# Table weights decoded by masks and predicated copies, and small inputs requested a stage earlier, in a four-layer fp32 kernel

## The chip, the cores and the metric

The kernel runs as one program on one core of one Trainium2 chip. The metric is the device time of the whole program in microseconds (us). Engines: TensorE (PE, its weight loads are PEld), VectorE (DVE), ScalarE (ACT), GpSimd (POOL) and SyncE (SP, which issues most of the transfers). They run in parallel, each takes its own instructions in order, and they wait for each other on semaphores.

## What is computed

A stack of four layers on x, 1024 tokens of 256 numbers in fp32. Each layer is a feed-forward, an attention and the feed-forward again, each behind a layer norm:

```python
x = x + 0.5 * _L0_ffn_ref(_layernorm(x), lut, gate_idx, up_idx, down_idx)
x = x + _L0_attn_ref(_layernorm(x), ...)          # 16 heads of 16, (q.k)^4, causal
x = x + 0.5 * _L0_ffn_ref(_layernorm(x), ...)
# layer 1: mixture of 8 experts, latent attention;  layer 2: mixture of 64 experts, gated delta rule
# layer 3: 4-bit feed-forward with 1024 hidden, attention on pooled keys

def _ghost_linear(x, idx, lut):
    w = lut[idx]                                   # lut has 16 entries
    return jnp.einsum('bsh,oh->bso', x, w)
gate = _ghost_linear(x, gate_idx, lut)             # gate_idx, up_idx [688, 256]
up = _ghost_linear(x, up_idx, lut)
h = jax.nn.silu(gate) * up
return _ghost_linear(h, down_idx, lut)             # down_idx [256, 688]
```

The weights of layer 0's feed-forward are thus given as integers from 0 to 15 and a table of 16 numbers. In layer 2's attention a small projection (`Wa`, `Wb`, with biases) gives the decay and the step size of each head and token, and then 16 heads are computed one after another, each with its own 512 KB of weights and a short convolution. Layer 3's attention multiplies keys with two pooling vectors, picks its heads by a matrix of head rows and pools windows of 16 keys by a window matrix.

## The kernel before

The tokens are 8 tiles of 128. The program is a series of stages (`Stage`); at the end of each all engines meet at a barrier, and the next stage's instructions, its transfers on SP among them, start behind it. A transfer issued inside a stage is therefore waited for inside that stage, unless it was issued by an earlier stage into a buffer that outlives it (`prefetch` of `norm_stage`, `idle` of the feed-forward stages, `AttentionWeights.load`).

**Layer 0, first feed-forward** (`l0_decode_ffn_stage`). The 688 hidden columns are cut into 6 units of 115 (padded). A unit's weights are 716 columns on 128 partitions: 460 for gate and up (`IN0`), 256 for down. They are decoded from the integers `idx` while earlier units are multiplied. For each of the 16 table entries VectorE makes the entry's value where the integer equals it and zero elsewhere (lines 460 and 474, `is_equal` then `mult`, 96 of them), and adds two or three of such results (lines 487 and 490, 51 adds). TensorE sums the 7 to 10 terms of a unit with the identity as weights (line 384, `decode`) in PSUM, and ScalarE copies the sum into `w` (line 437, `keep`). The products of a unit are `up` (line 395, gate and up of one half of the tokens), silu on ScalarE (line 445), `mix` on VectorE (line 498) and `down` (line 402). The order is written out by hand: up half 0, decode, up half 1, decode, down half 0, decode, down half 1. The decoded `w` is used again by the second feed-forward of the layer.

**Layer 0, attention.** After the head norm, `turn_stage` transposes q and k (line 656) and copies them out with a scale and a shift per partition, `columns` (lines 669 and 682), requested by the stage itself. The stage of the heads requests the matrix `own` (head rows) itself and multiplies it into the keys (line 1007).

**Layer 2, attention.** A norm, then `l2_decay_stage` (requests `w` and `row` at lines 2021 and 2022; its 16 products at line 2032 wait for both; then a chain of sigmoid, exp, ln and sums up to the table of decays), then `l2_heads_stage`, which requests gain and offset, the convolution taps and the weights of heads 0 and 1 and the first row of decays (lines 2251 to 2266) at its own start; line 2296 is its projection, 2528 and 2529 bring it to SBUF, line 2875 on GpSimd needs the row of decays.

**Layer 3, attention.** `l3_attention`'s last stage requests `taste`, `rows` and `inside` (lines 3662 to 3664); lines 3759 on GpSimd and 3780 on VectorE wait for all three.

## Time and profile before

| | |
|---|---|
| median of 3 runs | 2238.65 us (2233.58 to 2244.4) |
| the profiled execution, its own time | 2245.68 us |
| its span in the profile | 2244.0 us |
| PE busy | 1899.6 us, 85% |
| DVE, ACT, POOL busy | 1234.8, 840.0 and 471.7 us |
| granted TensorE clock, mean | 0.91 |

The span runs from the first to the last instruction; the profiled execution took 1.7 us more than it, and lies 7 us above the median. Shares of the span are means over many stages with different limits, so each stage has to be read by itself. A group of rows gives the time that instructions of one line were busy, the mean of one, and the idle time of the engine just before them with what ended it. "issue" there means that nothing the profile shows was waited for. The granted clock is 1.00 at TensorE's full 2.4 GHz and 0.50 at 1.2 GHz.

### The profile page before, as it was taken

To read this page: it belongs to the slowest core of one execution; us is meant where nothing else is said; L and a number is where in the kernel's file an instruction comes from. 1 tells how busy PE (TensorE), PEld (TensorE's weight loads), DVE (VectorE), ACT (ScalarE), POOL (GpSimd) and SP (SyncE) were. 2 spreads that over 40 slices of the span, in tenths; PEclk is the share of its full clock that TensorE was granted. 3 is DMA by queue.
4 is the path that set the end of the run, shared out by engine and by line. 5 is a ranking of instruction groups with operands and counts; after the bars stand their busy time and mean duration, and the time that the engine had idled before them with its cause. 6 is when DMAs were issued, how large, how long until landed. Compare 5 with 4: busy or idle time off the path is not lost. (4 is left out here: it accounts for less than half of the span.)

```text
span 2244.0 us, 52270 instructions
## 1 busy us (share of the span) xinstructions
PE 1899.6 (85%) x21231; PEld 1311.7 (58%) x21233; DVE 1234.8 (55%) x3231; ACT 840.0 (37%) x1977; POOL 471.7 (21%) x536
## 2 busy tenths in 40 slices
PE   7996779895999896676899999999998797679569
PEld 3444654563777563553666766676676674446456
DVE  7957641434663446644566666676666326542642
ACT  1013321221652222233667667767765202220120
POOL 0002410321000332641121222122121003720200
PEclk9997999996999997787999999999999697789679
DMA  7000000422400516761010001001000317730000
GB/s 267 13 0 1 1 1 0 154 68 89 179 1 3 189 38 206 234 229 41 21 41 22 21 22 41 21 22 41 22 30 14 84 26 232 247 149 7 3 3 19
DMA packets 55330, 157.37 MB, mean 70 GB/s; under 512 B 12899, under 2 KB 29881, under 8 KB 50822
## 3 DMA queue, kind: packets, MB, share of 16 engines
q1 hardware_dynamic: 45206, 128.84, 17.3%
q0 software_dynamic: 9888, 25.20, 3.4%
q8 instruction: 171, 2.80, 0.5%
q14 instruction: 65, 0.53, 0.1%
HBM read 115.36 MB, written 40.48 MB: 69 GB/s over the span
## 5 line engine op out<-in xcount | busy, mean ns | idle before, releaser
L2296 PE MATMUL l_heads_ps_p<-xnT,l2a_w 128*128 128x512 f32 x512 | 260.9, 625 | 22.0 <-DMA l2a_w<-in_l_w_heads 8.2
L2702 DVE SCALAR_TENSOR_TENSOR l_heads_taps<-l_heads_padded,l_heads_conv,l_heads_taps 128x1024 f32<-128x1024 f32 x144 | 187.5, 1321 | 11.0 <-ACT l_heads_taps L2529 10.0
L2296 PEld LDWEIGHTS l_heads_ps_p<-xnT,l2a_w 128*128 128x128 f32 x512 | 85.8, 191 | 83.9 <-issue 50.3
L198 PE MATMUL norm_turn<-zeros,ident 128*128 128x512 f32 x120 | 68.2, 726 | 52.9 <-PEq L60 52.9
L2875 POOL TENSOR_TENSOR l_heads_e<-l2a_table,l_heads_row 128x512 f32<-128x512 f32 x32 | 33.4, 1044 | 330.9 <-DVE l_heads_first L2713 325.7
L189 ACT ACT_TABLE_LOAD x10 | 12.8, 1283 | 205.3 <-PEq L60 205.3
L198 PEld LDWEIGHTS norm_turn<-zeros,ident 128*128 128x128 f32 x120 | 26.9, 233 | 88.3 <-issue 88.3
L2528 ACT COPY l_heads_padded<-l_heads_ps_p 128x512 f32<-128x512 f32 x96 | 57.2, 596 | 53.3 <-PE l_heads_ps_p L2296 53.3
L2529 ACT ACTIVATE l_heads_taps<-l_heads_ps_p,l_heads_conv 128x512 f32<-128x512 f32 x96 | 76.8, 800 | 0.0
L1905 ACT ACTIVATE l_heads_e<-l_heads_logit,l_heads_shift 128x128 f32<-128x128 f32 (+1 forms) x128 | 56.6, 443 | 44.6 <-DVE l_heads_shift L1937 44.6
L2878 POOL TENSOR_SCALAR_AFFINE_SELECT l_heads_e<-l_heads_e 128x512 f32<-128x512 f32 x64 | 67.6, 1056 | 9.8 <-POOL l_heads_e L2875 0.6
L384 PE MATMUL l_ffn_a_ps_w<-l_ffn_a_term,ident 128*128 128x512 f32 (+1 forms) x180 | 59.9, 479 | 9.0 <-DVE l_ffn_a_term L487 9.0
L2713 DVE SCALAR_TENSOR_TENSOR l_heads_first<-l_heads_bank,l2a_table,l_heads_e 128x128 f32<-128x128 f32 x128 | 36.0, 344 | 52.6 <-issue 46.1
L2330 PE MATMUL l_heads_bank<-l_heads_mt,l_heads_mz 32*32 32x32 f32 x3072 | 49.9, 194 | 13.9 <-issue 13.8
L2875 POOL TENSOR_TENSOR l_heads_e<-l_heads_row,l2a_table 128x512 f32<-128x512 f32 x32 | 34.4, 1074 | 118.7 <-DVE l_heads_qk L2755 118.7
L384 PEld LDWEIGHTS l_ffn_a_ps_w<-l_ffn_a_term,ident 128*128 128x128 f32 x180 | 33.8, 195 | 40.4 <-issue 28.5
L1019 DVE TENSOR_TENSOR l_heads_fourth<-l_heads_squares 128x768 f32<-128x768 f32 x32 | 31.0, 968 | 35.8 <-POOL l_heads_squares L915 35.8
L2330 PEld LDWEIGHTS l_heads_bank<-l_heads_mt,l_heads_mz 32*32 32x32 f32 x3072 | 41.5, 107 | 15.5 <-issue 15.4
L2603 ACT ACTIVATE l_heads_k_end<-l_heads_bank,l2a_table 128x128 f32<-128x128 f32 x128 | 36.8, 376 | 35.5 <-PE l_heads_bank L2436 35.5
L1937 DVE CUSTOM_DVE_ANT_0 l_heads_logit<-l_heads_ps_s,l_heads_mask 128x256 f32<-128x256 f32 (+1 forms) x128 | 40.3, 353 | 16.6 <-PE l_heads_ps_s L1837 16.5
L2773 DVE TENSOR_SCALAR l_heads_on<-l_heads_o,l_heads_mean_var,l_heads_rstd 128x128 f32<-128x128 f32 x128 | 35.6, 342 | 21.7 <-POOL l_heads_rstd L2888 21.2
L979 ACT ACTIVATE l_heads_squares<-l_heads_ps_s 128x768 f32<-128x768 f32 x32 | 26.0, 811 | 55.7 <-PE l_heads_ps_s L931 55.7
(706 smaller groups left out, 4868.9 us busy)
## 6 DMA issues: line engine op xcount, KB each, us to landing
l_results<-zeros SPq DMA_DIRECT2D x24, 512.0 KB, 5.3
l_ffn_a_w_in<-in_l_in_w SPq DMA_DIRECT2D x8, 1536.0 KB, 10.4
l_ffn_b_w_in<-in_l_in_w SPq DMA_DIRECT2D x8, 1536.0 KB, 11.1
l2a_w<-in_l_w_heads SPq DMA_DIRECT2D x16, 512.0 KB, 3.8
l_heads_row<-l_rows SPq DMA_DIRECT2D x16, 512.0 KB, 5.1
l_ffn_a_w_out<-in_l_out_w SPq DMA_DIRECT2D x8, 768.0 KB, 9.2
l_ffn_a_w_in<-l_results SPq DMA_DIRECT2D x8, 768.0 KB, 7.0
l_ffn_b_w_out<-in_l_out_w SPq DMA_DIRECT2D x8, 768.0 KB, 9.4
```

Source lines behind the costliest of these rows:

```text
L198: pe.matmul(turn[:, i % KC, (i // KC) % HALVES, :], core.ident[:], core.zeros[:, 0:HALF], start=True, stop=True)
L384: mm = pe.matmul(bank[:, 0:at.stop - at.start], core.ident[:], term[n % SLOTS][:, at], start=(m == 0), stop=(m == len(operands(u)) - 1))
L1905: act.activation(e[m % 4][:, lo:hi], logit[m % 4][:, lo:hi], ACT.Exp, bias=shift[:, m % 4, j:j + 1], scale=-1.0, accum_out=total[:, n % 4, ...
L1937: dve.tensor_tensor_reduce(logit[m % 4][:, lo:hi], score_bank(n, j)[:, i * width:(i + 1) * width], mask[:, 2 * P - width:], -1.0, LARGEST, ...
L2296: mm = pe.matmul(ps_p[half][:], w[b][:, which, c, :], core.xnT[:, c, half * HALF:(half + 1) * HALF], start=(c == 0), stop=(c == KC - 1))
L2330: mm = pe.matmul(bank[c][1][q, s, 0:BK], m_first(c, s)[q, q] if n == 1 else mz[c][q, s, 0, :], mt[c][q, s, :], start=True, stop=True)
L2528: act.copy(padded[which][:, 2 * half:2 * half + 2, PAD:], src)
L2529: act.activation(taps[which][:, 2 * half:2 * half + 2, :], src, ACT.Identity, bias=conv[b][:, which, TAPS:TAPS + 1], scale=conv[b][:, whic ...
L2603: last = act.activation(dst[:, s, :], tile_of_bank[name][:, s, :], ACT.Copy, scale=columns(h, column, c)[:, s:s + 1])
L2702: dve.scalar_tensor_tensor(out=taps[which][:], in0=padded[which][:, :, j:j + SEQ], scalar=conv[p % 2][:, which, j:j + 1], in1=taps[which][ ...
L2875: pool.tensor_tensor(m[:], a, b, ALU.subtract).then_inc(gap_ready, 1)
L2878: pool.affine_select(out=m[:], in_=m[:], compare_op=(ALU.is_gt, ALU.is_ge)[which], fill=DONE_BEFORE, base=0, pattern=[[0, SY], [-sign, P]] ...
```

## The change

**Decoding.** The table lookup is now a tree of choices on half a unit (358 columns), so there are 12 steps `v`. ScalarE folds the integer three times (lines 470, 474 and 478, absolute value of itself less a constant), makes an integer of all ones or zero from the last fold (`odd`, line 485), and three masks into PSUM (lines 493, 499 and 503, relu, nonzero where the choice falls the other way). VectorE makes 8 leaves: each is a pair of neighbouring table entries, chosen by the last bit with `and` and `xor` on the bits (line 547). Then 7 predicated copies join them: 4 by the outer mask, 2 by the high one, 1 by the tall one (line 562), and the last result lies in `w`. The identity products, the copies out of PSUM and the terms are gone. The two PSUM banks that held the sums now hold the masks, and the last half unit's gate and up use them. The padding entry is now 0 and `down` reads 113 rows of the last unit. TensorE's order is up half 0, down half 1 of the unit before, up half 1, down half 0; its first product of a unit waits for both steps of it.

**Requests.** A class `Asked` holds small tensors, their semaphore and their load; `columns` and `own` of layer 0, gates' weights and bias, gain and offset, and the first two heads' taps and weights of layer 2, and the three small tensors of layer 3 are now issued one stage or more ahead: in the first feed-forward of layer 0, in the norm before layer 2's decay stage, and in the first feed-forward of layer 3. The first row of decays stays where it was, in the stage of the heads.

```diff
+LEAVES = LUT // 2
+def folded_bits(entry):
+    first = abs(entry - (LUT - 1) / 2)
+    second = abs(first - LUT / 4)
+    third = abs(second - LUT / 8)
+    return entry >= LUT // 2, first < LUT / 4, second < LUT / 8, third < LUT / 16
...
             def up(u, h):
-                pe.wait_ge(w_ready, 2 * (u + 1))
-                if 2 * u + h >= 1:
+                pe.wait_ge(joined, joined_by(2 * u + 1))
+                if 2 * u + h >= 1 and banks(u, h) is not ps_mask:
                     pe.wait_ge(hidden_ready, 2 * u + h)
...
             for u in range(UNITS0):
-                more = u + 1 < UNITS0
                 up(u, 0)
-                if more:
-                    decode(u + 1, 0)
+                if u > 0:
+                    down(u - 1, 1)
                 up(u, 1)
...
+            def fold_index(v):
+                if v % 2 == 0:
+                    act.wait_ge(idx_loaded[v // 2], 32)
+                if v > 0:
+                    act.wait_ge(mask_ready[HIGH], v)
+                act.activation(fold[0][:], idx[:, v // 2, columns(v)], ACT.Abs, bias=middle).then_inc(folded, 1)
...
+            def make_leaves(v):
+                dve.wait_ge(odd_ready, v + 1)
+                if v > 0:
+                    dve.wait_ge(joined, joined_by(v - 1))
+                for k in range(LEAVES):
+                    set_entry = 2 * k if folded_bits(2 * k)[3] else 2 * k + 1
+                    other = 4 * k + 1 - set_entry
+                    dve.tensor_scalar(leaf_of(v, k).bitcast(I32), odd[v % 2][:], flips[:, k:k + 1],
+                                      table[:, other:other + 1].bitcast(I32), ALU.bitwise_and, ALU.bitwise_xor)\
+                        .then_inc(leaf_ready, 1)
+            def join(v, wanted):
...
+                    dve.copy_predicated(leaf_of(v, into), mask(bit).bitcast(I32), leaf_of(v, taken)).then_inc(joined, 1)
...
             for u in range(UNITS0):
-                more = u + 1 < UNITS0
-                if more:
-                    make_terms(u + 1, 0)
-                mix(u, 0)
...
+                for h in range(HALVES):
+                    v = 2 * (u + 1) + h
+                    if v < STEPS:
+                        make_leaves(v)
+                        join(v, OUTER)
+                    mix(u, h)
+                    if v < STEPS:
+                        join(v, HIGH)
+                        join(v, TALL)
...
+class Asked:
+    def __init__(self, nc, ctx, name, shapes):
+        self.at = [ctx.enter_context(nc.sbuf_tensor(f"{name}_{tensor}", shape, F32)) for tensor, shape in shapes]
+        self.loaded = nc.alloc_semaphore(f"{name}_loaded")
+        self.all = 16 * len(shapes)
+    def load(self, sp, *sources):
+        for at, source in zip(self.at, sources):
+            sp.dma_start(at[:], source).then_inc(self.loaded, 16)
...
+                def load_first(sp):
+                    gates.load(sp, w_gates.rearrange("(c p) n -> p c n", p=P), b_gates.partition_broadcast(P))
+                    first_w.load(sp, conv, conv_heads, w, w_heads)
+                    affine.load(sp, ln_w.rearrange("(d a) -> d a", a=1), ln_b.rearrange("(d a) -> d a", a=1))
+                norm_stage(nc, core, prefetch=load_first)
+                l2_decay_stage(nc, core, gates, table, rows)
```

VectorE in the first feed-forward of layer 0, before, between two `mix` instructions (`l_ffn_a_hidden`); `l_ffn_a_term` and `l_ffn_a_second` are looked-up values of a whole unit:

```order
L498 TENSOR_TENSOR l_ffn_a_hidden_217<-l_ffn_a_gate,l_ffn_a_ps_up 115x512 [waits l0_ffn_a_silu_done_217]
L460 TENSOR_SCALAR l_ffn_a_term_217<-l_ffn_a_idx,l_ffn_a_table 128x716 [waits l0_ffn_a_term_summed_217]
L460 TENSOR_SCALAR l_ffn_a_second_217<-l_ffn_a_idx,l_ffn_a_table 128x716 [waits l0_ffn_a_term_ready_217]
L490 TENSOR_TENSOR l_ffn_a_term_217<-l_ffn_a_term_217,l_ffn_a_second_217 128x716 [waits l0_ffn_a_looked_up_217]
L460 TENSOR_SCALAR l_ffn_a_second_217<-l_ffn_a_idx,l_ffn_a_table 128x716 [waits l0_ffn_a_term_ready_217]
L487 TENSOR_TENSOR l_ffn_a_term_217<-l_ffn_a_term_217,l_ffn_a_second_217 128x716 [waits l0_ffn_a_added_217,l0_ffn_a_looked_up_217]
L460 TENSOR_SCALAR l_ffn_a_term_217<-l_ffn_a_idx,l_ffn_a_table 128x716 [waits l0_ffn_a_term_summed_217]
L460 TENSOR_SCALAR l_ffn_a_second_217<-l_ffn_a_idx,l_ffn_a_table 128x716 [waits l0_ffn_a_added_217]
L487 TENSOR_TENSOR l_ffn_a_term_217<-l_ffn_a_term_217,l_ffn_a_second_217 128x716 [waits l0_ffn_a_looked_up_217]
L498 TENSOR_TENSOR l_ffn_a_hidden_217<-l_ffn_a_gate,l_ffn_a_ps_up 115x512 [waits l0_ffn_a_silu_done_217]
```

The same engine and place now, again from one `mix` to the next; `l_w` is the leaf that ends as the weights, `l_ffn_a_ps_mask` a mask in PSUM:

```order
L568 TENSOR_TENSOR l_ffn_a_hidden_217<-l_ffn_a_gate,l_ffn_a_ps_up 115x512 [waits l0_ffn_a_silu_done_217]
L562 COPY_PREDICATED l_w<-l_ffn_a_ps_mask_217,l_ffn_a_leaf_217 128x358 [waits l0_ffn_a_joined_217,l0_ffn_a_mask_ready1_217]
L562 COPY_PREDICATED l_ffn_a_leaf_217<-l_ffn_a_ps_mask_217,l_ffn_a_leaf_217 128x358 [waits l0_ffn_a_joined_217,l0_ffn_a_mask_ready1_217]
L562 COPY_PREDICATED l_w<-l_ffn_a_ps_mask_217,l_ffn_a_leaf_217 128x358 [waits l0_ffn_a_joined_217,l0_ffn_a_mask_ready0_217]
L547 TENSOR_SCALAR l_w<-l_ffn_a_odd_217,l_ffn_a_flips,l_ffn_a_table 128x358 [waits l0_ffn_a_joined_217,l0_ffn_a_odd_ready_217]
L547 TENSOR_SCALAR l_ffn_a_leaf_217<-l_ffn_a_odd_217,l_ffn_a_flips,l_ffn_a_table 128x358 x7
L562 COPY_PREDICATED l_w<-l_ffn_a_ps_mask_217,l_ffn_a_leaf_217 128x358 [waits l0_ffn_a_leaf_ready_217,l0_ffn_a_mask_ready2_217]
L562 COPY_PREDICATED l_ffn_a_leaf_217<-l_ffn_a_ps_mask_217,l_ffn_a_leaf_217 128x358 [waits l0_ffn_a_leaf_ready_217,l0_ffn_a_mask_ready2_217] x3
L568 TENSOR_TENSOR l_ffn_a_hidden_217<-l_ffn_a_gate,l_ffn_a_ps_up 115x512 [waits l0_ffn_a_silu_done_217]
```

A wait of VectorE for TensorE's sums (`term_summed`) is gone, and 15 instructions of 358 columns stand between two `mix`, where 8 of 716 stood here (12.5 on average over a unit's two halves).

TensorE in the same stage, before, from one pair of gate and up (line 395) to the next:

```order
L395 MATMUL l_ffn_a_ps_gate<-xnT,l_w 115x512 x2
L395 MATMUL l_ffn_a_ps_up<-xnT,l_w 115x512 x2
L384 MATMUL l_ffn_a_ps_w_217<-l_ffn_a_term_217,ident 128x512
L384 MATMUL l_ffn_a_ps_w_217<-l_ffn_a_term_217,ident 128x204
L384 MATMUL l_ffn_a_ps_w_217<-l_ffn_a_term_217,ident 128x512
L384 MATMUL l_ffn_a_ps_w_217<-l_ffn_a_term_217,ident 128x204
L402 MATMUL l_ffn_a_ps_down_217<-l_ffn_a_hidden_217,l_w 128x512 x2
L384 MATMUL l_ffn_a_ps_w_217<-l_ffn_a_term_217,ident 128x512
L384 MATMUL l_ffn_a_ps_w_217<-l_ffn_a_term_217,ident 128x204
L384 MATMUL l_ffn_a_ps_w_217<-l_ffn_a_term_217,ident 128x512
L384 MATMUL l_ffn_a_ps_w_217<-l_ffn_a_term_217,ident 128x204
L402 MATMUL l_ffn_a_ps_down_217<-l_ffn_a_hidden_217,l_w 128x512 x2
```

And now:

```order
L431 MATMUL l_ffn_a_ps_gate<-xnT,l_w 115x512 [waits l0_ffn_a_hidden_ready_217,l0_ffn_a_joined_217]
L431 MATMUL l_ffn_a_ps_gate<-xnT,l_w 115x512
L431 MATMUL l_ffn_a_ps_up<-xnT,l_w 115x512 x2
L439 MATMUL l_ffn_a_ps_down_217<-l_ffn_a_hidden_217,l_w 128x512 [waits l0_ffn_a_hidden_ready_217]
L439 MATMUL l_ffn_a_ps_down_217<-l_ffn_a_hidden_217,l_w 128x512
```

No identity product is left between them; what TensorE waits for at the start of a unit is the last predicated copy.

## Rows read from the trace of the kernel before

**Rows 1.** Busy time by engine, middle of the first feed-forward stage; columns: us, PE, PEld, DVE, ACT, POOL, granted clock, DMA share, GB/s.

```profile
40.00:130.00 90.00, 90.00 (x249) 44.89 (x248) 82.30 (x127) 9.24 (x18) 0.00 (x0) 1.00 0.20 79
```

**Rows 2.** Groups by line, 20 to 148.2 us; columns: xcount, busy us, mean ns, idle before.

```profile
L384 PE MATMUL l_ffn_a_ps_w<-l_ffn_a_term,ident 128*128 128x512 f32 (+1 forms) x180 | 59.9, 479 | 9.0 <-DVE l_ffn_a_term L487 9.0
L487 DVE TENSOR_TENSOR l_ffn_a_term<-l_ffn_a_term,l_ffn_a_second 128x716 f32<-128x716 f32 x41 | 37.1, 904 | 1.4
L460 DVE TENSOR_SCALAR l_ffn_a_second<-l_ffn_a_idx,l_ffn_a_table 128x716 f32<-128x716 int32 x51 | 29.9, 586 | 0.0
L395 PE MATMUL l_ffn_a_ps_gate<-xnT,l_w 128*115 128x512 f32 x48 | 22.7, 595 | 2.4 <-DVE l_ffn_a_hidden L498 1.5 <-ACT l_w L437 0.9
L498 DVE TENSOR_TENSOR l_ffn_a_hidden<-l_ffn_a_gate,l_ffn_a_ps_up 115x512 f32<-115x512 f32 x12 | 8.3, 688 | 17.7 <-ACT l_ffn_a_gate L445 17.4
```

**Rows 3.** Timeline, end of that stage; columns: start us, length us.

```profile
137.77 1.94 PE L395 MATMUL l_ffn_a_ps_gate<-xnT,l_w 128*115 128x512 f32 x4 [1.50 <-DVE l_ffn_a_hidden L498]
...
141.27 3.60 PE L402 MATMUL l_ffn_a_ps_down<-l_ffn_a_hidden,l_w 115*128 115x512 f32 x8
...
146.71 1.28 DVE L520 SCALAR_TENSOR_TENSOR x<-l_ffn_a_ps_w,x 128x512 f32<-128x512 f32 x2
```

**Rows 4.** Timeline of VectorE at the start of that stage.

```profile
20.62 0.59 DVE L460 TENSOR_SCALAR l_ffn_a_term<-l_ffn_a_idx,l_ffn_a_table 128x716 f32<-128x716 int32 x1 [6.22 <-DMA l_ffn_a_idx<-in_l_out_idx]
21.13 0.59 DVE L460 TENSOR_SCALAR l_ffn_a_second<-l_ffn_a_idx,l_ffn_a_table 128x716 f32<-128x716 int32 x1
21.75 0.91 DVE L487 TENSOR_TENSOR l_ffn_a_term<-l_ffn_a_term,l_ffn_a_second 128x716 f32<-128x716 f32 x1
22.57 0.59 DVE L474 TENSOR_SCALAR l_ffn_a_term<-l_ffn_a_idx,l_ffn_a_table 128x716 f32<-128x716 int32 x1
```

**Rows 5.** Single lines with operands per partition: shortest/median/longest ns.

```profile
L180 DVE TENSOR_SCALAR norm_xn<-x,norm_mean_var,norm_rstd x64: 401/407/414, 9.3 to 2182.5; 128x256 f32<-128x256 f32 x64
...
L2773 DVE TENSOR_SCALAR l_heads_on<-l_heads_o,l_heads_mean_var,l_heads_rstd x128: 336/341/348, 1133.3 to 1772.2; 128x128 f32<-128x128 f32 x128
...
L3544 ACT ACTIVATE l_ffn_a_hidden<-l_ffn_a_ps_up,l_ffn_a_bias x8: 687/687/688, 2019.5 to 2041.6; 128x512 f32<-128x512 f32 x8
```

**Rows 6.** Busy time and granted clock around two pauses of TensorE in layer 2.

```profile
1220.40:1222.10 1.70, 0.10 (x12) 0.00 (x0) 0.62 (x3) 1.70 (x4) 0.00 (x0) 1.00 0.00 0
1222.10:1223.80 1.70, 1.38 (x42) 0.93 (x43) 0.69 (x3) 1.38 (x5) 0.00 (x0) 1.00 0.04 10
...
1307.10:1308.80 1.70, 0.10 (x14) 0.00 (x0) 0.42 (x2) 1.70 (x4) 0.00 (x0) 1.00 0.00 0
1308.80:1310.50 1.70, 1.68 (x34) 0.89 (x35) 1.10 (x3) 1.03 (x4) 0.00 (x0) 0.82 0.05 10
```

**Rows 7.** Timeline, layer 0: turn stage and start of the heads.

```profile
210.24 3.65 PE L656 MATMUL l_turn_bank<-ident,l0a_qk 128*128 128x128 f32 x16 [9.19 <-PEq L60]
213.66 1.53 DVE L682 TENSOR_SCALAR l0a_qkT<-l_turn_bank,l_turn_columns 128x512 f32<-128x512 f32 x2 [4.23 <-DMA l_turn_columns<-in_l_affine]
...
219.59 2.86 DVE L1007 TENSOR_SCALAR l_heads_own_k<-l0a_qkT,l_heads_own 128x1024 f32<-128x1024 f32 x4 [2.27 <-DMA l_heads_own<-in_head_rows]
```

**Rows 8.** Timeline, layer 2: decay stage and start of the heads.

```profile
1025.58 0.38 SPq L2021 DMA_DIRECT2D decay_w<-in_l_w_gates  x1
...
1028.93 7.04 PE L2032 MATMUL decay_ps<-decay_w,xnT 128*128 128x32 f32 x32 [4.75 <-DMA decay_row<-in_l_b_gates]
...
1046.07 0.33 SPq L2251 DMA_DIRECT2D l_heads_gain<-in_l_ln_w  x1
...
1050.86 15.48 PE L2296 MATMUL l_heads_ps_p<-xnT,l2a_w 128*128 128x512 f32 x32 [8.17 <-DMA l2a_w<-in_l_w_heads]
...
1052.97 1.04 POOL L2875 TENSOR_TENSOR l_heads_e<-l2a_table,l_heads_row 128x512 f32<-128x512 f32 x1 [5.21 <-DMA l_heads_row<-l_rows]
```

**Rows 9.** Timeline, layer 3: start of the heads.

```profile
2104.37 0.33 SPq L3662 DMA_DIRECT2D l_heads_taste<-in_l_pool  x1
...
2107.75 0.29 DVE L3780 TENSOR_TENSOR l_heads_term<-l3a_qk,l_heads_taste 128x128 f32<-128x128 f32 x1 [4.06 <-DMA l_heads_inside<-in_l_window]
```

More of the change, by code:

```diff
@@ L359, in l0_decode_ffn_stage, with columns, leaf_of, mask @@
         block = st.block()
+        middle, quarter, eighth, above_tall, above_high, above_outer = (shift[:, i:i + 1] for i in range(6))
+        def columns(v):
+            return slice(v % 2 * PART, (v % 2 + 1) * PART)
+        def leaf_of(v, k):
+            return w[:, v // 2, columns(v)] if k == ROOT else leaf[k - (k > ROOT)][:]
+        def mask(bit):
+            return mask_of[bit][:, 0:PART]
+        def joined_by(v, bit=0):
+            return len(JOINS) * v + sum(PER_BIT[bit:])
+        def banks(u, h):
+            return ps_mask if (u, h) == (UNITS0 - 1, 1) else (ps_gate, ps_up)
         @block.sync
@@ new lines, in silu @@
+            def silu(u, h):
+                act.wait_ge(up_done, 2 * u + h + 1)
+                if 2 * u + h >= 1:
+                    act.wait_ge(hidden_ready, 2 * u + h)
+                act.activation(gate[:], banks(u, h)[0][0:F0, :], ACT.Silu).then_inc(silu_done, 1)
+            act.wait_ge(shifts_ready, 6)
+            fold_index(0)
+            make_odd(0)
+            for v in range(2):
+                make_mask(v, OUTER)
+                make_mask(v, HIGH)
+                fold_index(v + 1)
+                make_odd(v + 1)
+                make_mask(v, TALL)
@@ L448, in _ @@
+                    if v + 1 < STEPS:
+                        fold_index(v + 1)
+                        make_odd(v + 1)
+                    silu(u, h)
+                    if v < STEPS:
+                        make_mask(v, TALL)
             for h in range(HALVES):
```

295 lines of the change are left out of this document (142 added, 153 removed).

## The prediction

> **What bounds the kernel now.** I read the stages one by one, first by busy time in a stretch, then by groups, then by the timeline at their ends. In the middle of the first feed-forward TensorE is busy for all of 90 us and VectorE for 82.3 [rows 1]: TensorE sets the pace, VectorE is close behind. Of TensorE's work 59.9 us are identity products (line 384), that is decoding; VectorE decodes too, in 96 lookups of 586 ns and 51 additions of 904 ns, and waits for no product there except in the gaps before a mix [rows 2]. So the stage can only get shorter if both engines lose decoding work. It runs from 20.62 us [rows 4] to 146.71 + 1.28 = 147.99 us [rows 3]. For the requests I read where an engine's idle time ends in a DMA just behind a barrier: five places, below.
>
> **Part A, the decoding.** TensorE loses all 180 identity records, 59.9 us. Its rest for half a unit is gate, up and down; gate and up together take 141.27 - 137.77 = 3.50 us, down half of that, 1.75 [rows 3], so 5.25 us per half unit, 63 us in all. VectorE now has 12 steps of 8 leaves and 7 predicated copies on 358 columns, and the 12 mixes as before. It will be the longer one, so its price decides.
>
> A leaf is a two-operation instruction with two operands per partition. Such a one took 407 ns on 256 columns and 341 on 128 [rows 5], 0.51 ns per column; 358 columns give 407 + 102 x 0.51 = 459 ns. Independent instructions overlap by 586 - 510 = 0.08 us (starts 20.62 and 21.13 [rows 4]), so one every 0.38 us. Low bound: the lookup took 586 ns on 716 columns, less 358 x 0.51 is 403, so 0.32. High bound: if `and` and `xor` on integers go one column per cycle, as the addition does ((904 - 688) / (716 - 512) = 1.06 ns per column [rows 2]), a leaf costs 358 x 0.55 = 0.20 more, 0.58. I take 0.38: it is also an instruction of one streamed input, both sides in SBUF.
>
> No predicated copy is in this trace. It streams a mask from PSUM and data from SBUF, like the mix (688 ns, one input in PSUM) and the addition; at their slope it takes 904 - 358 x 1.06 = 525 ns, one every 0.44 us behind the overlap (starts 21.75 and 22.57, 0.91 long). Low bound 0.25, at the leaves' slope. High bound 0.82: the old value of the destination is a third stream, and if it needs a second pass that is 0.38 more. I take 0.44, the nearest rows; where a copy waits for the one just before it (the tall one, and the next step's first leaf) its full length counts, 0.56 with the semaphore.
>
> A step is 8 x 0.38 + 4 x 0.44 (outer) + 0.44 + 0.56 (high) + 0.56 (tall) = 6.36 us; 12 are 76.3. Ten mixes lie between, 0.61 each, 6.1. The first leaf waits for four dependent instructions of ScalarE: one takes 687 ns on 512 columns with an operand per partition [rows 5], by columns alone 0.48 on 358, so between the two; I take 0.57 (estimate), 2.3 us behind the integers' arrival at 20.62, so 22.9. ScalarE's 7 small instructions and a silu per step are under 4.5 us beside 7 and stay covered; if they weren't, each step would grow by the difference. The last weights are then joined at 22.9 + 76.3 + 6.1 = 105.3.
>
> Two waits come on top. The first gate and up starts with the low clock, as TensorE stands still from the norm on; it then takes some 5.2 us, not 3.5, and VectorE reaches the mix at 4.9 with silu to follow: 1.1 us lost. Later, gate and up plus silu are done 3.5 + 0.1 + 0.7 = 4.3 us (silu by the activation in [rows 5]) into a step, and VectorE comes to the mix at 8 x 0.38 + 4 x 0.44 = 4.8: just covered. But per unit TensorE has 10.5 us of work in 14, with one pause of 3 us. After pauses of about the same length, 0.10 us busy in 1.7, the granted clock stayed at 1.00 in one place and fell to 0.82 and lower in the next in another [rows 6]; with 3 us I expect it to fall in about three of five units, and at 1.2 GHz silu comes 1.2 us late for the mix: 3.6 us. So the weights are ready at 110.0.
>
> Behind that come two gate and up, three down, 2 x 3.50 + 3 x 1.75 = 12.2 us, without a wait since the last half uses the mask banks, and the end of the stage (transposes, addition), 147.99 - (137.77 + 3.50 + 3.50) = 3.2 us [rows 3]. The stage ends at 125.5, or with one slow clock at 126: **22 us earlier**.
>
> The Trainium skill (VectorE: DVE Perf Modes, the section on the TRN2 errata) speaks against this edit: SBUF operands cost a fixed time per instruction, and it advises tiles of at least 512 elements. The change makes 180 instructions of 358 columns out of 147 of 716. The rows agree that there is such a fixed part: a lookup's 586 ns has some 220 that no column explains [rows 2]; it is in the sum above through the rows, and the columns saved are worth more.
>
> **Part B, the requests.** (1) Turn stage: the copy waited for the scales until 213.66, 4.23 us [rows 7]. But the transposes before it run at the low clock, 16 records in 3.65 us, and had not gone much further: four banks are filled by 213.9 and the other four need about 2 us more. The copies would end about 216.7 instead of 217.3: 0.6 us, not 4. (2) `own` saves up to 2.27 - 0.7 us, and GpSimd's fill of v's ones lies beside it then: 1.3. (3) Decay stage: products start with the stage at 1025.6, not 1028.93: 3.3. They also took 7.04 us for 32 small records at the low clock [rows 8], after a pause of 4.75 us; with a pause of 1.5 some may run at the high one, 0 to 3.5 less, I take 1.5. What follows is a chain of ScalarE and VectorE with no cover, so all of it counts. (4) Heads of layer 2: the projection starts at 1046.1, not 1050.86: 4.7, less 0.2 for the row of decays, which is issued as first now but still lands some 5 us after the barrier [rows 8]; GpSimd's exponents are ready by the time ScalarE asks. 4.5. (5) Layer 3: VectorE starts at 2104.4, not 2107.75: 3.3 [rows 9]. Sum 0.6 + 1.3 + 3.3 + 1.5 + 4.5 + 3.3 = **14.5 us**. The ends are 10 (the decay products unchanged, half of 4 eaten by the row) and 18. The transfers themselves: SP issues 8 in layer 2's norm at 0.33 to 0.38 us or somewhat more each [rows 8], 3 to 4 us, nothing is queued behind them but the barrier; in layer 0 two tiny ones stand behind the integers and ahead of weights that are needed 100 us later; layer 3's follow a feed-forward's weights. No added wait has anything new behind it.
>
> **Sum.** 22 + 14.5 = 36.5 us. On the profiled execution 2245.7 - 36.5 = 2209.2, its span 2207.5. That execution lies 7 us above the median, so from the median: 2238.65 - 36.5 = **2202 us**. What this measurement can tell from no change is about 0.5%, 11 us.
>
> **The rivals.**
> *Leaves at one column per cycle.* For it: the operation is on bits, and no row has one. Against: every one-input instruction in SBUF shown runs at the faster slope. 96 x 0.20 = 19 us, 2221.
> *Predicated copies in two passes.* For it: three streams. Against: the mix reads PSUM and SBUF in one. 84 x 0.38 = 32 us, 2234, which is within 0.5% of before.
> *Requests that bring half.* The turn stage shows how a wait ends where the next is already due; if the row of decays and the clock do so too, 7 us less: 2209.
> *Slower than before.* VectorE as the bound of the decoding stage: both prices at their high ends, 51 us, and TensorE then pauses some 7 us in every unit, so that it starts each at the low clock, which costs little more as VectorE leads: 2238.65 - 36.5 + 51 = 2253, and 2256 with the clock. It decides from 36.5 / 84 = 0.43 us above my price of a predicated copy, 0.87 us each. ScalarE's 7 instructions would have to cost over 0.9 us each to do the same, and no row of that size comes near.
> *The clock.* The Trainium skill (TensorE: Matmul & The Clock Gate, on oscillation) has it that a kernel which waits between groups of products can start every group throttled. By that rule all five units lose 1.2 us and the tail 1.7, not 3.6 and 0.5 together: 2206. The other way, never throttled, is 2198.
>
> **How the numbers follow.** Forecast, with the clock either way and the requests as priced, 0.62; requests half, 0.09; slow leaves alone 0.12; two-pass copies 0.09, of which I count 0.07 as within 0.5% and 0.02 as faster; slower 0.08, of which 0.06 is beyond 0.5%. Faster by over 0.5%: 0.62 + 0.09 + 0.12 + 0.02 = 0.85. Within 0.5%: 0.07 + 0.02 = 0.09. Slower: 0.06. The range has the leaves' low bound and an unthrottled clock on one side (2202 - 6 - 4 = 2192) and a little of the copies' low bound, whose whole 84 x 0.19 = 16 us I don't include as no row of two inputs has such a slope, so 2189; on the other stand slow leaves with some clock loss, 2226; beyond lie the two-pass copies.
>
> **What would show it.** In the profile after: the last copy into `l_w` near 110 us and the next norm's start near 126; line 547 at about 460 ns and line 562 at about 525; TensorE's granted clock between 0.8 and 1 from 40 to 110 us with idle before line 431 released by line 562; no DMA among the releasers at the turn, decay and head stages; the first projection of layer 2's heads within 0.5 us of its barrier. Wrong would be a predicated copy near 0.9 us, a leaf near 0.65, ScalarE named as releaser of the leaves, or waits of the same length on the row of decays.

## The result and the profile after

The changed kernel took 2214.61 us, the median of 4 runs (2210.26 to 2214.98); the kernel before took 2238.98 (4 runs). The medians lie 24 us apart, 1.1%. The ratio on record, which is not the quotient of the medians, is 0.9865, 95% interval 0.9834 to 0.9895, or 30 us: faster, by 24 to 30 us. The forecast was 2202 us in a range of 2189 to 2226. The profiled execution of the changed kernel ("after" below) took 2214.98 us, its span is 2213.2 us.

Between the two profiled executions lie 30.8 us of span. I read where they arise from the start of each layer-norm, since every stage ends in a barrier: 17.0 us in the decode stage (the next norm starts at 131.79 us, not 148.81), nothing in layer 0's attention, 8.4 in layer 2's attention, 5.6 from layer 3's attention to the end. Of the stages in between, layer 2's first feed-forward is 2.3 us longer and the others differ by less than 1 us.

Busy time by engine in the middle of the decode stage; the columns are those of [rows 1].

```profile
40.00:110.00 70.00, 55.30 (x111) 21.62 (x111) 62.32 (x144) 38.81 (x70) 0.00 (x0) 0.90 0.26 102
```

TensorE was busy for all of [rows 1]; now it is for 55.3 of 70 us, at a mean granted clock of 0.90, and VectorE leads with 62.3. The groups from 20 to 131 us, as [rows 2]:

```profile
L547 DVE TENSOR_SCALAR l_ffn_a_leaf<-l_ffn_a_odd,l_ffn_a_flips,l_ffn_a_table 128x358 int32<-128x358 int32 x84 | 32.7, 464 | 0.0
L431 PE MATMUL l_ffn_a_ps_gate<-xnT,l_w 128*115 128x512 f32 x44 | 27.5, 760 | 40.5 <-DVE l_w L562 38.7 <-DVE l_ffn_a_hidden L568 1.7
L562 DVE COPY_PREDICATED l_ffn_a_leaf<-l_ffn_a_ps_mask,l_ffn_a_leaf 128x358 f32<-128x358 int32 x48 | 23.7, 549 | 0.0
L562 DVE COPY_PREDICATED l_w<-l_ffn_a_ps_mask,l_ffn_a_leaf 128x358 f32<-128x358 int32 x36 | 20.1, 557 | 1.2
L568 DVE TENSOR_TENSOR l_ffn_a_hidden<-l_ffn_a_gate,l_ffn_a_ps_up 115x512 f32<-115x512 f32 x11 | 7.5, 682 | 11.9 <-ACT l_ffn_a_gate L510 11.9
```

The 180 identity products and the 51 additions are gone. A leaf is 464 ns, a predicated copy 549 to 557. TensorE waits 38.7 us for VectorE's copies, 22.5 of it ahead of the first unit; VectorE waits for silu (line 510) ahead of its mix. A gate product is 760 ns on the mean, not 595, as the granted clock was lower behind the pauses (below). One step of VectorE in the timeline, from the mix ahead of it to its own:

```profile
56.75 0.67 DVE L568 TENSOR_TENSOR l_ffn_a_hidden<-l_ffn_a_gate,l_ffn_a_ps_up 115x512 f32<-115x512 f32 x1
57.34 0.56 DVE L562 COPY_PREDICATED l_w<-l_ffn_a_ps_mask,l_ffn_a_leaf 128x358 f32<-128x358 int32 x1
57.79 0.55 DVE L562 COPY_PREDICATED l_ffn_a_leaf<-l_ffn_a_ps_mask,l_ffn_a_leaf 128x358 f32<-128x358 int32 x1
58.44 0.56 DVE L562 COPY_PREDICATED l_w<-l_ffn_a_ps_mask,l_ffn_a_leaf 128x358 f32<-128x358 int32 x1
59.11 0.47 DVE L547 TENSOR_SCALAR l_w<-l_ffn_a_odd,l_ffn_a_flips,l_ffn_a_table 128x358 int32<-128x358 int32 x1
59.49 2.73 DVE L547 TENSOR_SCALAR l_ffn_a_leaf<-l_ffn_a_odd,l_ffn_a_flips,l_ffn_a_table 128x358 int32<-128x358 int32 x7
...
63.89 0.68 DVE L568 TENSOR_TENSOR l_ffn_a_hidden<-l_ffn_a_gate,l_ffn_a_ps_up 115x512 f32<-115x512 f32 x1
```

From mix to mix 7.14 us. An independent copy starts 0.45 us after the last (57.34, 57.79); one that needs the last one's result starts 0.65 after it (57.79, 58.44), and the next step's first leaf 0.67 after that. TensorE's starts behind an idle time, in brackets:

```profile
36.19 3.76 PE L431 MATMUL l_ffn_a_ps_gate<-xnT,l_w 128*115 128x512 f32 x4 [22.53 <-DVE l_w L562]
...
51.92 1.97 PE L431 MATMUL l_ffn_a_ps_gate<-xnT,l_w 128*115 128x512 f32 x4 [3.23 <-DVE l_w L562]
...
66.19 2.60 PE L431 MATMUL l_ffn_a_ps_gate<-xnT,l_w 128*115 128x512 f32 x4 [3.24 <-DVE l_w L562]
81.70 3.76 PE L431 MATMUL l_ffn_a_ps_gate<-xnT,l_w 128*115 128x512 f32 x4 [3.24 <-DVE l_w L562]
98.57 3.44 PE L431 MATMUL l_ffn_a_ps_gate<-xnT,l_w 128*115 128x512 f32 x4 [3.23 <-DVE l_w L562]
113.84 2.45 PE L431 MATMUL l_ffn_a_ps_gate<-xnT,l_w 128*115 128x512 f32 x4 [3.24 <-DVE l_w L562]
```

All five pauses inside the loop are 3.2 us. Behind one the four products took 1.97 us, behind the four others up to 3.76. The granted clock (last but two) in a window around the start at 81.70 and in the last unit:

```profile
80.60:86.00 5.40, 4.30 (x5) 1.72 (x6) 5.19 (x13) 3.33 (x6) 0.00 (x0) 0.54 0.01 3
...
113.80:119.10 5.30, 5.26 (x9) 2.13 (x10) 0.00 (x0) 0.00 (x0) 0.00 (x0) 0.68 0.00 0
```

0.54 is nearly all at the lower level, 1.2 GHz. Silu is late behind such a start, and the mixes of the first halves of units 0 to 4 wait 1.34, 0, 1.11, 2.47 and 0.86 us, 5.8 in all. The end of the stage, for [rows 3], and the stages that part B was to help, for [rows 7 to 9]:

```profile
129.65 1.28 DVE L595 SCALAR_TENSOR_TENSOR x<-l_ffn_a_ps_mask,x 128x512 f32<-128x512 f32 x2
131.79 2.38 DVE L172 BATCH_NORM_STATS2 norm_stats<-x 128x6 f32<-128x256 f32 x7 [0.86 <-PEq L60]
...
200.43 0.31 POOL L989 MEMSET l0a_v<- 128x128 f32 x1 [30.61 <-POOLq L60]
200.48 4.40 DVE L1086 TENSOR_SCALAR l_heads_own_k<-l0a_qkT,l0a_columns_own 128x1024 f32<-128x1024 f32 x4 [0.73 <-PEq L60]
200.60 1.75 POOL L990 MEMSET l0a_v<- 128x1920 f32 x1
...
203.04 0.67 PE L1009 MATMUL l_heads_ps_s<-l0a_qkT,l_heads_own_k 128*128 128x256 f32 x2 [4.14 <-DVE l_heads_own_k L1086]
...
1009.13 6.68 PE L2107 MATMUL decay_ps<-l_gates_w,xnT 128*128 128x32 f32 x32 [1.47 <-PEq L60]
...
1025.98 15.95 PE L2362 MATMUL l_heads_ps_p<-xnT,l2a_w 128*128 128x512 f32 x32 [3.43 <-PEq L60]
...
1029.61 1.04 POOL L2941 TENSOR_TENSOR l_heads_e<-l2a_table,l_heads_row 128x512 f32<-128x512 f32 x1 [1.77 <-DMA l_heads_row<-l_rows]
...
2077.55 0.42 DVE L3862 TENSOR_TENSOR l_heads_term<-l3a_qk,l3a_rows_taste 128x128 f32<-128x128 f32 x1 [0.72 <-PEq L60]
```

In these stages no DMA is a releaser any more but for the row of decays. In layer 0, however, the four own_k multiplications start at once and take 4.40 us, not 2.86: TensorE's first scores come 2.6 us behind the barrier, as before.

### The profile page after: what moved, and what is told of

The parts are those of the page before. It is cut to its first block and busy times, and to the rows that moved or that the text cites. A ratio compares the mean times of both kernels' runs of the same rounds, so it can differ in the third digit from the quotient of the medians.

```text
span 2213.2 us, 52159 instructions
## 1 busy us (share of the span) xinstructions
PE 1847.7 (83%) x21053; PEld 1275.8 (58%) x21053; DVE 1218.2 (55%) x3265; ACT 879.8 (40%) x2049; POOL 473.0 (21%) x542
## 5 line engine op out<-in xcount | busy, mean ns | idle before, releaser
L2362 PE MATMUL l_heads_ps_p<-xnT,l2a_w 128*128 128x512 f32 x512 | 266.3, 636 | 20.5 <-ACT l_heads_shaped L2681 8.1
L2768 DVE SCALAR_TENSOR_TENSOR l_heads_taps<-l_heads_padded,l2a_conv,l_heads_taps 128x1024 f32<-128x1024 f32 x144 | 187.9, 1323 | 9.7 <-ACT l_heads_taps L2595 8.9
L2595 ACT ACTIVATE l_heads_taps<-l_heads_ps_p,l2a_conv 128x512 f32<-128x512 f32 x96 | 76.7, 799 | 0.0
L431 PE MATMUL l_ffn_a_ps_gate<-xnT,l_w 128*115 128x512 f32 x44 | 27.5, 760 | 40.5 <-DVE l_w L562 38.7
L2016 DVE CUSTOM_DVE_ANT_0 l_heads_logit<-l_heads_ps_s,l_heads_mask 128x256 f32<-128x256 f32 (+1 forms) x128 | 40.3, 353 | 16.3 <-PE l_heads_ps_s L1916 16.2
L2025 DVE COPY l_heads_eT<-l_heads_ps_t 128x384 f32<-128x384 f32 x64 | 32.7, 553 | 25.7 <-PE l_heads_ps_t L1925 24.4
```

Source lines behind the costliest of these rows:

```text
L2016: dve.tensor_tensor_reduce(logit[m % 4][:, lo:hi], score_bank(n, j)[:, i * width:(i + 1) * width], mask[:, 2 * P - width:], -1.0, LARGEST, ...
L2362: mm = pe.matmul(ps_p[half][:], w[b][:, which, c, :], core.xnT[:, c, half * HALF:(half + 1) * HALF], start=(c == 0), stop=(c == KC - 1))
L2595: act.activation(taps[which][:, 2 * half:2 * half + 2, :], src, ACT.Identity, bias=conv[b][:, which, TAPS:TAPS + 1], scale=conv[b][:, whic ...
L2768: dve.scalar_tensor_tensor(out=taps[which][:], in0=padded[which][:, :, j:j + SEQ], scalar=conv[p % 2][:, which, j:j + 1], in1=taps[which][ ...
```

## Experiments

Each ratio is against the kernel before, run on the same chip as the kernel. The three sets ran on three chips of unlike speed (before: 2279, 2240 and 2243 us), so ratios are compared, not times. The first set is part A and B alone, warm and late_mix; the second the changed kernel again, late_ones, best and the prices; the third the rest. late_ones and the prices have one execution each and so no ratio.

| kernel | ratio, 95% interval | next norm starts at (us) | own_k x4 (us) | decay products (us) |
|---|---|---|---|---|
| part A alone, twice | 0.9904 (0.9877–0.9930), 0.9937 (0.9913–0.9960) | 131.3, 133.7 | 2.89, 2.89 | 7.04, 7.04 |
| part B alone, twice | 0.9935 (0.9915–0.9955), 0.9949 (0.9931–0.9968) | 148.0, 149.5 | 4.41, 4.40 | 5.18, 5.56 |
| changed, twice more | 0.9893 (0.9867–0.9919), 0.9889 (0.9868–0.9910) | 134.2, 135.2 | 4.40, 4.39 | 4.99, 6.09 |
| warm | 0.9851 (0.9825–0.9878) | 124.5 | 4.39 | 6.30 |
| late_mix | 0.9812 (0.9788–0.9836) | 123.4 | 4.40 | 5.10 |
| late_ones | none (2217.03 us) | 130.7 | 2.74 | 6.01 |
| best | 0.9809 (0.9784–0.9834) | 121.6 | 2.74 | 5.92 |
| best_first | 0.9844 (0.9817–0.9871) | 121.8 | 2.74 | 5.84 |

**The two halves.** Each kernel has one half of the change: the decode stage alone, or the requests alone.

> The kernel before with the new decode stage alone; all requests stay where they were. Theory (the two halves of the change add up): the first layer-norm after the decode stage starts 17 us earlier than in the kernel before (at 131.8 us instead of 148.8), nothing later changes, and the median falls by 17 us (ratio .992). Rival (the decode stage gave less than the profiled pair shows, because the profiled execution of before lay 7 us above its median): the median falls by only 10 us (ratio .9955).

> The kernel before with the moved requests alone; its decode stage is the old one. Theory (adds up): the decode stage ends at 148 us as before, the turn stage of layer 0 is .75 us shorter, the layer-2 heads come 8 us earlier, layer 3's heads 3.3 us earlier, and the median falls by 12 us (ratio .9945). Rival (most of what the profiled pair showed behind the decode stage was the difference of two executions): the stage-by-stage gains that the requests can explain, .75 + 4.5 + 3.6 + 3.3 less what the longer layer-2 conv gives back, are seen in the trace, but the median falls by only 7 us (ratio .997).

The decode stage alone gave its 17 us in the trace (131.26), and a ratio of 0.9904, 22 us; the requests alone gave 0.9935, 15 us. Both rivals, smaller gains in the whole time, are out. Their product, 0.984, was better than the whole kernel's first ratio, 0.9865. So the whole was run again on another chip:

> The changed kernel itself, once more, beside the kernel before on the same chip. Theory (the two halves add up: .9904 and .9935 alone make .984): ratio .984, the stage of part A ends 17 us earlier in the trace, and the .9865 of the first measurement lay at the upper part of its interval. Rival (the halves take from each other, as part A's earlier end was partly paid back later): ratio .9865 or more.

0.9893, against the theory of 0.984: the rival's number. To know whether the halves take from each other or chips differ, all three ran once more on one chip.

> The new decode stage alone, again, on one chip with the three others of this set. Theory (its gain is what the traces show, 14.6 to 18 us by how often TensorE's clock falls in the pauses): ratio .992 to .9935. Rival (the first measurement, .9904, is right, and 4 us come from somewhere that the traces of single executions do not show): ratio .9905 or less.

> The moved requests alone, again. Theory (.75 us in the turn stage, 0 in the layer-0 heads, 8 to 10 in layer-2 attention, 3.3 in layer 3): ratio .994 to .9945. Rival: the first measurement, .9935, was right and the whole change falls short of the product of its halves for a reason of its own.

> The changed kernel a third time, beside its two halves. Theory (the halves add up): the ratio is the product of the two halves' ratios on this chip within .003, some .987. Rival (they take from each other): .003 or more above the product.

0.9937 x 0.9949 = 0.9886 and the whole 0.9889: the halves add up. Both halves gave a little less than their theories said, and part A's 0.9904 did not come again. The first set's chip was the odd one. There the two expert feed-forwards of layer 2, which the change does not touch, took 172 to 181 us from norm to norm, on the other chips 156 to 166. The ratios of each half on the two chips overlap in their intervals, so it isn't shown that the halves gained more on it, and no run of the whole change on that chip was made.

**The clock in the pauses.** In the decode stage, TensorE's part:

```diff
+            pe.wait_ge(joined, joined_by(0))
+            keep_warm(3)          # matmul(ps_gate, ident, zeros[:, 0:HALF])
             for u in range(UNITS0):
...
                 down(u, 0)
+                if u + 1 < UNITS0:
+                    pe.wait_ge(silu_done, 2 * u + 2)
+                    keep_warm(3)
```

> The changed kernel with three multiplications of zeros by the identity in each pause of TensorE's loop (3.2 us, in front of a unit's first gate and up), and three in front of the first gate and up. Theory (the clock falls behind each of these pauses, and what is left of the stalls hangs on it): the granted clock is 1.00 in the four first gate/ups that showed .54 to .76, their 5.2 us fall to 3.5 to 3.8; the stalls of VectorE go from 5.8 us to under 1.5, the last gate and up from 5.22 to 3.5 us; the stage ends 5 to 6 us earlier. Rival (the clock falls whatever TensorE does there, as it is low elsewhere behind dense work): the three take 5.2 us instead of 2.6 after the fall and push the gate and up back: the stage ends 0 to 8 us later.

The theory holds, and the gain is somewhat larger than it said. The group of gate products (line 431) and of the added ones (446) in this run, in the columns of [rows 2]:

```profile
L431 PE MATMUL l_ffn_a_ps_gate<-xnT,l_w 128*115 128x512 f32 x44 | 23.2, 653 | 6.2 <-DVE l_w L571 3.7 <-DVE l_ffn_a_hidden L577 2.5
...
L446 PE MATMUL l_ffn_a_ps_gate<-zeros,ident 128*128 128x512 f32 x36 | 18.5, 653 | 16.7 <-DVE l_w L571 15.9 <-ACT l_ffn_a_gate L519 0.8
```

From 50 us on every window shows a granted clock of 1.00. One stall of 1.05 us is left, the first; the stage is 7.3 us shorter than in the first profile of after. The rule of the Trainium skill that the prediction weighed (TensorE: Matmul & The Clock Gate, on oscillation), that groups behind a wait can each start throttled, points the right way. The trace of after agrees for four of the loop's five pauses and spared one; in the seven executions with this loop 31 of 35 pauses of 3.2 us were followed by slow products (2.44 to 3.76 us for the four), and 4 were not (1.97).

**The order of the mix.** In VectorE's loop:

```diff
                         join(v, OUTER)
+                        join(v, HIGH)
                     mix(u, h)
                     if v < STEPS:
-                        join(v, HIGH)
                         join(v, TALL)
```

> The changed kernel with VectorE's product of gate and up moved behind the two joins by the second mask of a step, ahead of the join by the third. Theory (the 5.8 us of stalls in front of the product are a matter of order, the silu comes up to 2.5 us after VectorE reaches the product): two joins, 1.1 to 1.3 us, now lie in front; the stalls of 1.34, 1.11 and .86 us are gone and the one of 2.47 shrinks to 1.2, and the last dependent join no longer follows its operand at once (.65 us pitch down to .55, .1 us in ten steps): the stage ends 5 to 6 us earlier, at 125 us, ratio to the changed kernel .9975. Rival (the product is late because TensorE's clock fell, and TensorE hands over later when it gets its input later): the stalls move on with the product, the stage gains 0 to 1.5 us.

More than the theory asked for. One boundary of a step, then TensorE's starts behind a pause, of which the first shown was slow:

```profile
77.46 0.55 DVE L562 COPY_PREDICATED l_w<-l_ffn_a_ps_mask,l_ffn_a_leaf 128x358 f32<-128x358 int32 x1
77.90 0.55 DVE L562 COPY_PREDICATED l_ffn_a_leaf<-l_ffn_a_ps_mask,l_ffn_a_leaf 128x358 f32<-128x358 int32 x1
78.34 0.68 DVE L568 TENSOR_TENSOR l_ffn_a_hidden<-l_ffn_a_gate,l_ffn_a_ps_up 115x512 f32<-115x512 f32 x1
78.93 0.55 DVE L562 COPY_PREDICATED l_w<-l_ffn_a_ps_mask,l_ffn_a_leaf 128x358 f32<-128x358 int32 x1
```

```profile
51.53 3.52 PE L431 MATMUL l_ffn_a_ps_gate<-xnT,l_w 128*115 128x512 f32 x4 [1.90 <-DVE l_w L562]
...
72.25 1.94 PE L431 MATMUL l_ffn_a_ps_gate<-xnT,l_w 128*115 128x512 f32 x4 [1.12 <-DVE l_ffn_a_hidden L568]
...
79.53 1.97 PE L431 MATMUL l_ffn_a_ps_gate<-xnT,l_w 128*115 128x512 f32 x4 [1.91 <-DVE l_w L562]
...
86.06 1.94 PE L431 MATMUL l_ffn_a_ps_gate<-xnT,l_w 128*115 128x512 f32 x4 [1.12 <-DVE l_ffn_a_hidden L568]
```

The mix hides one dependent copy's latency (6.91 us from mix to mix, not 7.14: 2.3 us in ten), and it hands over later, which splits TensorE's pause of 3.2 us into 1.9 and 1.1. From the third unit on the products behind those take 1.94 to 1.97 us each time and no mix waits: 4.6 us of stalls and 1.7 of the last unit come back. 2.3 + 4.6 + 1.7 = 8.6, and the stage is 8.4 us shorter. The rival, stalls that move on with the mix, is out. How the 4.6 us divide between the clock and the later mix, which by itself covers 1.1 us more of a late silu, this run doesn't separate: behind the one slow group (51.53) the mix waited 0.23 us, where in after the slow ones cost 0.86 to 2.47. No run has the changed kernel on this chip, so the 8.4 us are the trace's; warm, on the same chip, is at 0.9851, with an interval that overlaps.

**The fill beside own_k.** Two edits of the same cause: the fills wait for own_k, or lie in the turn stage (best, on top of late_mix).

```diff
# late_ones
+                pool.wait_ge(own_ready, ROWS)
                 pool.memset(v1[:, :, :, HEAD:HEAD + 1], 1.0).then_inc(ones_ready, 1)
...
-                pe.wait_ge(ones_ready, 2)      # now ahead of the first values
# best
-            turn_stage(nc, core, "l0_turn", qk, 2 * KC, qkT, asked)
+            turn_stage(nc, core, "l0_turn", qk, 2 * KC, qkT, asked, fill)
```

> The changed kernel, with GpSimd's two fills in the heads stage of layer 0 made to wait until VectorE's four own_k multiplications are done. Theory (shared port): the four take 2.9 us instead of 4.40, the first scores start 1.1 us after the stage's start (2.6 before); but the fills end about 5 us after it, and the first triangle mask on GpSimd then comes .5 to 1 us behind its data, so .5 to 1 us of the 1.5 remains. Rival (not the fills but the earlier start itself, at once behind the stage's barrier, is what slows the four): they take 4.4 us still.

> The changed kernel with the product behind the second mask's joins, as in the run late_mix, and with GpSimd's two fills of v's ones and zeros (.31 and 1.75 us) in the turn stage of layer 0, where GpSimd has nothing else, instead of beside VectorE's four own_k multiplications. Theory (the four took 4.40 us instead of 2.86 since the fills ran beside them on a port that both use): they take 2.9 us, TensorE's first scores start 1.0 to 1.3 us after the stage's start instead of 2.6, the heads gain 1.3 to 1.6 us, the turn stage is not longer since VectorE reads PSUM there with idle time in front of each; with the 8.4 us of late_mix the ratio is .9805. Rival (the fills are as much in the way in the turn stage, or the four are slow for another reason): the heads gain nothing, ratio .981 to .982, or the turn stage is 1 to 1.5 us longer.

Start of the heads of layer 0 in late_ones, then in best with the turn stage ahead of it:

```profile
199.24 2.74 DVE L1088 TENSOR_SCALAR l_heads_own_k<-l0a_qkT,l0a_columns_own 128x1024 f32<-128x1024 f32 x4 [0.73 <-PEq L60]
200.05 0.70 PE L1010 MATMUL l_heads_ps_s<-l0a_qkT,l_heads_own_k 128*128 128x256 f32 x2 [2.38 <-DVE l_heads_own_k L1088]
...
202.04 0.32 POOL L990 MEMSET l0a_v<- 128x128 f32 x1 [33.52 <-DVE l_heads_own_k L1088]
```

```profile
182.85 0.32 POOL L962 MEMSET l0a_v<- 128x128 f32 x1 [23.54 <-POOLq L60]
183.02 1.75 POOL L963 MEMSET l0a_v<- 128x1920 f32 x1
...
189.77 2.74 DVE L1095 TENSOR_SCALAR l_heads_own_k<-l0a_qkT,l0a_columns_own 128x1024 f32<-128x1024 f32 x4 [0.73 <-PEq L60]
190.67 0.67 PE L1018 MATMUL l_heads_ps_s<-l0a_qkT,l_heads_own_k 128*128 128x256 f32 x2 [2.48 <-DVE l_heads_own_k L1095]
```

The fills were the cause: own_k x4 takes 2.74 us in all three kernels without them beside it, 4.39 to 4.41 in all eight others with moved requests, 2.86 to 2.89 in the three where it waited for its DMA and only the fills' end lay beside it. But late_ones gained nothing by the end of the stage: from own_k to the next norm 106.0 us, as in after. GpSimd's first triangle mask stood behind the fills, 4.7 us from own_k's start (5.5 in after), and by the end even that was gone, not a part of it as expected. In best the mask comes at 3.4 instead of 5.3 to 5.8, and from own_k to the next norm are 101.4 and 102.9 us (best, best_first), 104.9 on the mean of the eight others.

The eight spread from 102.4 to 106.0 with TensorE's granted clock, which in the window from 80 to 100 us behind own_k's start was 1.00 in the shortest and 0.66 in the longest, so kernels have to be compared at one clock. At 0.74 there, the changed kernel in its two further runs and warm need 105.4, 105.4 and 105.5 us and best_first 102.9: 2.5 us, of which the earlier mask explains 2. best has the lowest ratio, 0.9809, its median 42 us below before's and 20 below the changed kernel's on the same chip; of the 19.1 us between the traces of those two, 15.7 lie ahead of the end of layer 0's attention, where the edits are. Its ratio is not to be told from late_mix's 0.9812, so the 2.5 us stand on the traces.

**Warming the first unit alone.** best, with the three products of zeros ahead of the first gate and up.

> The run best with three multiplications of zeros by the identity ahead of TensorE's first gate and up. Theory (the first gate and up is slow, 6.2 us with its up, because the engine stood idle for 22 us before it; the product behind it is .98 us late and the next .23): both at 1.00 of the clock, the two stalls gone, the stage ends 1 us earlier than best's, ratio .980. Rival (the three are themselves at the low clock, 5.2 us, and TensorE falls back in the 1.4 us that are left, or comes late): same time as best or up to 1 us later, ratio .981.

```profile
29.44 4.61 PE L446 MATMUL l_ffn_a_ps_gate<-zeros,ident 128*128 128x512 f32 x6 [15.91 <-DVE l_w L565]
36.05 3.41 PE L431 MATMUL l_ffn_a_ps_gate<-xnT,l_w 128*115 128x512 f32 x4 [2.00 <-DVE l_w L565]
```

The rival's case: the added products were slow themselves, and after 2.0 us of idling the first group of gate products took 3.41 us, hardly less than 3.76. The stall in front of the first mix was 0.24 us here and 0.38 in best, as the late mix covers most of it; the next norm starts at 121.79 and 121.58. Nothing gained. That the ratio is 0.9844 and not 0.9809 is no finding on this edit: the two ran on different chips.

**The prices by themselves.** VectorE alone, behind the kernel's end, six independent instructions of each kind on 128, 358 and 512 columns, and six chained copies.

```diff
+    run(lambda o: dve.tensor_scalar(o[:, 0:wide].bitcast(I32), bits[:, 0:wide], one[:, 0:1], one[:, 1:2], ALU.bitwise_and, ALU.bitwise_xor))
+    run(lambda o: dve.tensor_scalar(o[:, 0:wide], taken[:, 0:wide], onef[:, 0:1], onef[:, 1:2], ALU.mult, ALU.add))
+    run(lambda o: dve.copy_predicated(o[:, 0:wide], ps_mask[:, 0:wide].bitcast(I32), taken[:, 0:wide]))
+    run(lambda o: dve.copy_predicated(o[:, 0:wide], masks[:, 0:wide], taken[:, 0:wide]))
```

> The changed kernel with a stage behind its end in which VectorE alone works: six each of the leaf's form (two bitwise operations on int32, two per-partition operands), of the same form in float, of the predicated copy with its mask in PSUM and with its mask in SBUF, on 128, 358 and 512 columns, and six predicated copies that each take the last one's result. Theory (the copy goes at the pace that 716 columns in 904 ns and 512 in 682 ns of float sums show, 1.08 ns a column, wherever its mask lies): 300, 550 and 716 ns on 128, 358 and 512 columns, the same with the mask in SBUF; the leaf at half of that, 340, 464 and 550 ns; a dependent copy .65 us behind the last. Rival (a fixed price of reading PSUM is in the copy, and bitwise operations go at full pace with a small fixed part): with the mask in SBUF the copy takes 60 ns less, and the leaf 215, 464 and 630 ns, while the float form of it takes 340 to 550.

```profile
L646 DVE COPY_PREDICATED price_out<-price_masks,price_taken 128x512 f32<-128x512 int32 x6 | 3.7, 714 | 0.0
L644 DVE COPY_PREDICATED price_out<-price_ps_mask,price_taken 128x512 f32<-128x512 int32 x6 | 3.7, 712 | 0.0
L649 DVE COPY_PREDICATED price_out<-price_ps_mask,price_out 128x358 f32<-128x358 int32 x6 | 3.3, 557 | 0.2
...
L638 DVE TENSOR_SCALAR price_out<-price_bits,price_one 128x512 int32<-128x512 int32 x6 | 2.8, 538 | 0.0
...
L638 DVE TENSOR_SCALAR price_out<-price_bits,price_one 128x358 int32<-128x358 int32 x6 | 2.3, 460 | 0.0
L641 DVE TENSOR_SCALAR price_out<-price_taken,price_onef 128x358 f32<-128x358 f32 x6 | 2.3, 460 | 0.0
L638 DVE TENSOR_SCALAR price_out<-price_bits,price_one 128x128 int32<-128x128 int32 x6 | 1.6, 340 | 6.6 <-ACT price_ps_mask L623 6.6
...
L644 DVE COPY_PREDICATED price_out<-price_ps_mask,price_taken 128x128 f32<-128x128 int32 x6 | 1.3, 291 | 0.0
```

A copy costs (712 - 291) / 384 = 1.10 ns per column and 151 ns besides, wherever its mask lies; the leaf (538 - 340) / 384 = 0.52 and 274, the same as in float. The rival falls on each point, and so does one point of the theory: a chained copy starts 0.59 us after the last (3.52 us from the first start to the last end of six), less than the 0.65 in the kernel.

## Why the prediction held, and where it was off

The time lay in the range, and what was said to bound the stage was right. The gain was not: 36.5 us were forecast, and 24 to 30 measured. The time alone, 2214.6 us, lies between the times of two rivals, requests that bring half (2209) and slow leaves (2221); it is the rows that put both out.

**What bounds, and the prices.** As forecast, VectorE became the engine that leads and TensorE waits for it. A leaf 464 ns (459 forecast), a copy 549 to 557 (525). The low and high bounds of both are out, and with them three rivals: slow leaves, copies in two passes, slower than before.

**The step.** 6.36 us forecast; 6.53 and 6.61 in the trace, 7.14 with its mix instead of 6.97. The pace of independent instructions was right (0.38 and 0.44); what was mis-sized is the dependent copy, 0.65 us after its predecessor and not 0.56, and the leaf behind it, 0.67. With 0.2 us at the first leaf the steps and mixes were 2.5 us longer, in 12 steps.

**Stalls and clock.** Forecast 1.1 and 3.6 us, a fall in three of five units. Measured 5.8 us in the first profile, with falls behind four of five pauses, and 5.4 to 8.5 (mean 6.6) in seven executions with this stage. That the clock was the cause warm shows, which left the order as it was; late_mix got rid of the stalls by the order, without an added product. The tail took 17.15 us from the last copy (113.78) on, 1.7 of it by the clock, where at most 16 were forecast. First leaf 0.2, steps 2.5, stalls 1.1, tail 1.2: the stage ends at 130.93 us, not 126. Over the seven executions part A brings 13.6 to 18.1 us in the traces, mean 16.2, not 22. The mechanism was right, and its terms were too small: in the first profile the largest error is the steps (2.5 us, the dependent starts), over all seven executions the stalls come near it, 6.6 us where 4.7 were forecast, as the clock fell behind 31 of 35 pauses and not behind three of five.

**Requests.** Turn stage 0.75 us in the first two profiles (0.6 forecast), but that isn't shown to be the request's doing. Both executions of part A alone, which still ask for the scales in the stage, are as short: from its first transpose to its last copy 6.37 and 6.33 us, against 7.11 before and 6.14 to 6.62 with the moved request. There the scales landed sooner, and ScalarE, the first to need them, waited 2.54 us where it had waited 4.29:

```profile
194.55 0.78 ACT L744 ACTIVATE l0a_qkT<-l_turn_bank,l_turn_columns 128x512 f32<-128x512 f32 x1 [2.54 <-DMA l_turn_columns<-in_l_affine]
```

Own 0 (1.3): TensorE's first scores start 3.3 us behind the last copy of the turn stage before and after. The wait on the DMA became a contention with the fill, which the prediction saw beside it and priced at 0.3 us, where it took 1.5. Decay products: 7.04 us in all three executions with the old requests, 3.73 to 6.68 in the eleven with the new, mean 5.58, so 1.5 as forecast, though the first profile shows 0.4. Layer 2's attention as a whole took 827 us on the mean of three without the moved requests (825 to 829) and 818 of eleven with them (811 to 825): 9.0 us, with an uncertainty of some 3 as single executions differ by up to 14, where 3.3 + 1.5 + 4.5 = 9.3 were forecast. Layer 3's attention 102.3 and 99.2: 3.2 (3.3 forecast). Together 12.9 of 14.5, or 12.2 without the turn stage. The two ratios of part B alone are 15 and 11 us. "Requests that bring half", 7 us, is out.

**The sum.** 22 + 14.5 = 36.5 us stood against the first two profiles' 30.8, and against 24 in the medians. The profiled execution of before lay 7 us above its median, that of after at its own, so part of the 30.8 was the choice of execution. All three measurements of the change together are 0.9865, 0.9893 and 0.9889, some 26 us; by the medians 24, 22 and 25. The stages of the traces, 16.2 and 12.9 on the mean, make 29. So 7 us of the miss lie in the stages, 6 in part A and 1.6 in part B, and 3 to 6 more between the stages and the whole time; where these arise the runs don't show.
